# A cross-attention kernel on one core: image values and token norms move from the opening into step 11 of the first batch, and the spread of the image values over heads becomes four whole-row copies

## The reference

```python
text_ehs, ip_ehs = ctx[:, :-4], ctx[:, -4:]
q = heads(x @ W_q); k_t = heads(text_ehs @ W_k); v_t = heads(text_ehs @ W_v)
probs_t = softmax(q @ k_t.T * Dh**-0.5);  text_out = probs_t @ v_t
k_ip = heads(ip_ehs @ W_k_ip);  v_ip = heads(ip_ehs @ W_v_ip)
qsem = l2norm(probs_t @ text_ehs);  ip_n = l2norm(ip_ehs)
fused = q @ k_ip.T * Dh**-0.5 + 0.5 * (qsem @ ip_n.T)
probs_ip = softmax(fused) * spatial_mask[:, None]
out = (text_out + probs_ip @ v_ip) @ W_out + b_out + x
```

## Time and profile before

| what | value |
|---|---|
| time, median of 3 runs | 732.73 us (730.79 to 734.06) |
| profiled execution, its own time | 731.94 us |
| its span | 730.1 us |
| granted TensorE clock, mean | 0.997 of full speed |
| PE busy | 713.3 us (98%) |
| DVE, ACT, POOL busy | 634.2 (87%), 558.5 (76%), 422.1 us (58%) |
| chain of waits, by engine | PE 91%, DVE 2%, DMA 2% |

### The profile page before, as it was taken

The page is one execution under the profiler, slowest core; times in us unless marked ns, Lnnn a source line. Parts: engine busy times, 40 slices in busy tenths (PEclk is TensorE's granted clock), DMA queues, the critical chain, the costliest instruction groups (busy, mean ns, idle before and its releaser), DMA issues.

```text
span 730.1 us, 22544 instructions
## 1 busy us (share of the span) xinstructions
PE 713.3 (98%) x7221; PEld 560.9 (77%) x7221; DVE 634.2 (87%) x1878; ACT 558.5 (76%) x1595; POOL 422.1 (58%) x524
## 2 busy tenths in 40 slices
PE   8898999999999999999999999999999999999897
PEld 6577788787787878788787777878787887877665
DVE  5588998989889898988999898898989989898986
ACT  5478787877878788787877878787887878777772
POOL 7545646465564745656565565656556564654754
PEclk9999999999999999999999999999999999999999
DMA  9764372442536246263543436354352725325001
GB/s 277 164 142 99 79 140 73 83 125 45 120 75 135 74 62 144 41 128 75 107 104 58 105 80 133 76 88 113 51 117 73 142 71 92 64 43 123 13 1 22
DMA packets 136355, 68.57 MB, mean 94 GB/s; under 512 B 76672, under 2 KB 136112, under 8 KB 136240
## 3 DMA queue, kind: packets, MB, share of 16 engines
q1 hardware_dynamic: 131856, 64.05, 41.1%
q10 hardware_dynamic: 4064, 2.73, 1.3%
q0 software_dynamic: 320, 0.36, 0.4%
HBM read 40.38 MB, written 15.24 MB: 76 GB/s over the span
## 4 chain that ended last, share of the span: by engine, by line
PE 91%; DVE 2%; DMA 2%; ACT 1%; issue 1%; POOL 1%; SPq 0%; ACTq 0%; DVEq 0%; POOLq 0%
PE ps_gram L785 18%; PE ps_prep L673 18%; PE ps_pT L768 13%; PE ps_gram L786 12%; PE ps_score L760 6%; PE ps_prep L734 5%; PE ps_val L794 4%; PE ps_val L795 2%; PE ps_prep L731 1%; PE ps_prep L704 1%; PE ps_prep L706 1%; PE ps_prep L824 1%; PE ps_prep L835 1%; DMA w_raw<-in_L_xattn_W_k_ip 1%; DMA q_st<-q_bounce 1%
## 5 line engine op out<-in xcount | busy, mean ns | idle before, releaser
L592 POOL TENSOR_TENSOR dual<-prob 128x371 f32<-128x371 f32 (+1 forms) x288 | 251.3, 872 | 288.1 <-ACT prob L1043 288.1
L785 PE MATMUL ps_gram<-gram_hi,pT_hi 125*128 125x371 f16 (+1 forms) x864 | 272.3, 320 | 0.1
L786 PE MATMUL ps_gram<-gram_lo,pT_hi 125*128 125x371 f16 (+2 forms) x864 | 230.1, 267 | 0.0
L1037 ACT ACTIVATE pT_hi<-ps_pT 125x384 f16<-125x384 f32 (+1 forms) x288 | 138.9, 482 | 113.5 <-PE ps_pT L768 105.4
L1235 DVE TENSOR_TENSOR pT_lo<-ps_pT,pT_hi 125x384 f16<-125x384 f32 (+1 forms) x288 | 155.2, 539 | 33.0 <-ACT pT_hi L1037 28.2
L1027 ACT ACTIVATE prob<-ps_score,low 128x371 f32<-128x371 f32 (+1 forms) x288 | 165.3, 574 | 21.6 <-DVE low L1230 16.4
L1230 DVE TENSOR_REDUCE low<-ps_score 128x1 f32<-128x371 f32 (+1 forms) x288 | 154.9, 538 | 18.8 <-PE ps_score L760 13.7
L1248 DVE CUSTOM_DVE_ANT_0 quad_junk<-ps_gram,dual 128x371 f32<-128x371 f32 (+1 forms) x288 | 153.1, 532 | 4.5 <-PE ps_gram L786 1.6
L794 PE MATMUL ps_val<-val,pT_hi 125*128 125x84 f16 (+3 forms) x864 | 152.3, 196 | 0.0
L1043 ACT ACTIVATE prob<-prob 128x371 f16<-128x371 f32 (+1 forms) x288 | 151.5, 526 | 0.0
L768 PE MATMUL ps_pT<-ident,prob 128*125 128x128 f32 (+1 forms) x864 | 142.2, 273 | 6.5 <-ACT prob L1027 3.2
(11 more groups left out here) (264 smaller groups left out, 1468.4 us busy)
## 6 DMA issues: line engine op xcount, KB each, us to landing
ctx_sb<-in_ctx_t SPq DMA_DIRECT2D x15, 750.0 KB, 5.0
w_raw<-k_bounce SPq DMA_DIRECT2D x32, 216.0 KB, 4.0
k_st<-k_bounce SPq DMA_DIRECT2D x28, 216.0 KB, 3.8
k_bounce<-k_hi SPq DMA_DIRECT2D x15, 288.0 KB, 4.3
k_bounce<-k_lo SPq DMA_DIRECT2D x15, 288.0 KB, 4.4
q_st<-q_bounce SPq DMA_DIRECT2D x60, 63.0 KB, 2.4
xt_sb<-in_x_t SPq DMA_DIRECT2D x16, 168.0 KB, 4.7
w_raw<-k_hi SPq DMA_DIRECT2D x32, 84.0 KB, 3.1
```

The source lines that it names most:

```text
L592: nc.gpsimd.tensor_tensor(dual[0:r, t % 2, :], prob[0:r, g % 4, 0:TX], prob_16[0:r, t % 2, :], ALU.subtract).then_inc(s_dual, 1)
L785: nc.tensor.matmul(ps_gram[t % 2][:, 0:TX], hi, gh[0:TROWS[i], i, :], start=(i == 0), stop=False, skip_group_check=True)
L786: last = nc.tensor.matmul(ps_gram[t % 2][:, i * TC:TX], hi, gl[0:TROWS[i], i, i * TC:TX], start=False, stop=(i == NT - 1), skip_group_chec ...
```

## The change

- Opening: the loads of `W_v_ip`, of the token rows and of `W_out`, the clearing of `vip_diag`, the sums, the inverse root, the diagonal, the image values, the broadcast and the two copies are gone from it. One small reduction on DVE makes `own_head` (80 x 20: one where the head is the row's own).
- Batch 0: SP issues the three loads in step 1 (`W_v_ip` into a quarter of `w_raw` that `k_st` doesn't cover). DVE makes the sums in step 7, POOL the root in step 8, DVE the diagonal in step 9. In step 11 PE makes the broadcast and the image values between transposes and products, in `ps_prep[1]`, after piece 5 and ahead of piece 7 of the next batch; DVE copies them out ahead of its quadratic form. SP writes `vip_rows` to DRAM in step 12.
- The spread: four DMAs instead of 20. Each brings for 4 batches the whole rows of all heads into all 20 head places, 80 partitions of 5,120 bytes. They are issued in steps 16 and 17 of batch 0 and steps 1 and 5 of batch 1.
- POOL multiplies the rows of a batch with `own_head`, in place: batch 0 in step 7 of batch 1 (there it waits for all four spreads), batch n in its own step 8, batch 15 in step 9 of batch 14. `finish` waits for this in place of the spreads.

```diff
-VIP_AT = {9: 5, 10: 5, 11: 5, 13: 5}
+VIP_STEP, VIP_KEEP_STEP, IP_SUM_STEP, IP_ROOT_STEP, IP_DIAG_STEP, LATE_LOAD_STEP, VIP_OUT_STEP = 11, 8, 7, 8, 9, 1, 12
...
+VIP_AT = {(0, 16): 0, (0, 17): 1, (1, 1): 2, (1, 5): 3}
...
-            def spread_v_ip(h0, h1):
+            def spread_v_ip(i):
                 sp.wait_ge(s_vip_out, 16)
...
-                for h in range(h0, h1):
-                    sp.dma_start(vip_diag[h * NIP:(h + 1) * NIP, :, h * DH:(h + 1) * DH],
-                                 vip_view[:, :, h * DH:(h + 1) * DH]).then_inc(s_vip_in, 16)
+                sp.dma_start(vip_diag[:, rows_, :].rearrange("p b c -> p (b c)"),
+                             src.unsqueeze(0).to_broadcast([H, NIP, VIP_SLICE * C])).then_inc(s_vip_in, 16)
+
+            def late_loads():
+                load_rows(sp, wo_sb, w_out, s_wo)
...
+                sp.dma_start(w_v_ip_sb, w_v_ip.rearrange("(c p) n -> p c n", p=P)).then_inc(s_w[3], 16)
+                sp.dma_start(ip_rows[:, :], ip[:, :]).then_inc(s_ip, 16)
...
-            nc.gpsimd.memset(vip_diag[:, :, :], 0.0).then_inc(s_pool_set, 1)
...
+            def keep_own_head(n):
+                if n == 0:
+                    pool.wait_ge(s_vip_in, 16 * len(VIP_AT))
+                    pool.wait_ge(s_own_head, 1)
+                mine = vip_diag[:, n, :].rearrange("p (h d) -> p h d", d=DH)
+                nc.gpsimd.tensor_tensor(mine, mine, own_head[:, :].unsqueeze(2).to_broadcast([H * NIP, H, DH]), ALU.mult).then_inc(s_vip_own, 1)
...
                     end_early(b, t, prepare)
...
+                    if b.n == 1 and t == VIP_KEEP_STEP - 1:
+                        keep_own_head(0)
+                    if b.n and prepare and t == VIP_KEEP_STEP:
+                        keep_own_head(b.n)
...
-            pe.wait_ge(s_setup_ev, 2)
-            pe.wait_ge(s_w[3], 16)
-            for e in range(EC // 2):
-                v_ip(e)
             scores(start, 0)
             scores(start, 1)
-            for e in range(EC // 2, EC):
-                v_ip(e)
             transposes(start, 0)
             scores(start, 2)
-            pe.wait_ge(s_ipdiag, 1)
-            nc.tensor.matmul(ps_prep[1][0:S, 0:64], ones[:, :], ip_diag[:, :], start=True, stop=True).then_inc(s_setup_pe, 1)
+            def image_values():
+                pe.wait_ge(s_prep_lo, NM + VIP_BANK_PIECES_DONE)
+                pe.wait_ge(s_ipdiag, 1)
+                pe.wait_ge(s_w[3], 16)
+                nc.tensor.matmul(ps_prep[1][0:S, 0:64], ones[:, :], ip_diag[:, :], start=True, stop=True)
+                for e in range(EC):
+                    last = nc.tensor.matmul(ps_prep[1][0:64, 64:64 + C], ip_T[:, e, :], w_v_ip_sb[:, e, :], start=(e == 0), stop=(e == EC - 1))
+                last.then_inc(s_setup_pe, 1)
...
+                    if b.n == 0 and t == VIP_STEP:
+                        image_values()
                     products(b, t)
```

More of the change, by code:

```diff
@@ L474, in body @@
                         load_xt(b.next().next())
-                    if b.n == 0 and t == 0:
+                    if b.n == 0 and t == LATE_LOAD_STEP:
+                        late_loads()
+                    if b.n == 0 and t == VIP_OUT_STEP:
                         bring_v_ip()
-                    if b.n == 0 and t in VIP_AT:
-                        done = sum(VIP_AT[at] for at in VIP_AT if at < t)
-                        spread_v_ip(done, done + VIP_AT[t])
+                    if (b.n, t) in VIP_AT:
+                        spread_v_ip(VIP_AT[b.n, t])
                     if prepare and t == Q_OUT_STEP:
@@ L547, in _ @@
             split_lo(start, PIECE_X)
[L548 to L549 removed]
+            nc.gpsimd.memset(q_st[1][:, :, :], 0.0).then_inc(s_pool_set, 1)
             def residual(a):
@@ L1422, in body @@
                         split_wo()
+                    if b.n == 0 and t == IP_SUM_STEP:
+                        ip_sums()
+                    if b.n == 0 and t == IP_DIAG_STEP:
+                        ip_scale()
+                    if b.n == 0 and t == VIP_STEP:
+                        image_values()
                     softly(t, 1)
```

71 lines of the change are left out of this document (42 added, 29 removed).

## The result

| | before | after |
|---|---|---|
| time, median (lowest to highest), 11 runs each | 732.87 us (730.79 to 735.41) | 737.95 us (735.47 to 739.34) |
| ratio, 95% interval | | 1.0065 (1.0046 to 1.0084) |
| profiled execution, its own time and its span | 731.94, 730.1 us | 739.01, 737.2 us |
| granted clock, mean | 0.997 | 0.990 |
| PE busy | 713.3 us | 716.8 us |

The forecast was 731.4 us, "the same", in a range of 728.6 to 734.6. The changed kernel is slower by 5 us. The page's first part hardly tells it: PE has 3.5 us more of busy time and stands idle for some 3.6 us more (the span is longer by 7.1; rows 1 are the same line before).

What follows compares the result with a forecast made beforehand. PE, busy 98% of the span, was taken as the bound. The terms -1.5 - 1.27 + 1.0 + 0.5 + 0.4 gave -0.87, hence 731.1 or 731.9 by two bases; 731.4 us was taken, range 728.6 to 734.6.

Steps and rivals of the forecast that it cites:

- Term 6: POOL: multiplications hidden, but batch 0's waits in batch 1 for the last spread, landing about 102.7 us: plus 0.4 us.
- term 3: Opening: PE's low clock may reach past the start of products 0; plus 1.0 us, bounds 0 and 2.4.
- the third rival: Batch 1: last spread lands late, so POOL, `dual`, DVE and PE stand; +3.7 us, about 736; chance 0.08.
- Term 1: Opening: the query lands earlier with loads and clearing removed; minus 1.5 us, bounds 0 and 3.2.
- Term 2: Opening: the second half of the image values leaves the path, so transposes 0 start earlier; minus 1.27 us.
- the second rival: Opening gives nothing back: query only 0.5 us earlier, PE without filler at 1.2 GHz; +1.5 us, about 733.6; chance 0.22.
- up at 34: Opening: sign that the granted clock of 0.5 reaches past products 0's start and is up at 34 us.
- Term 4: Step 11 of batch 0: image values and broadcast take 2.55 us, mostly covered by 2.00 us idle; plus 0.5 us.
- Term 5: Batch 0: late loads on SP ahead of batch 1's query and keys, with a cover of 3.9 us; costs nothing.

Runs made afterwards that it cites:

- e7: Kernel before with only four whole-row spreads (steps 9, 10, 11, 13 of batch 0), POOL's multiplications and `own_head`, without clearing `vip_diag`; 732.60 us, ratio 0.9986.
- e5: Changed kernel plus 24 unread turns of the identity on TensorE in batch 1's idle time ahead of the transposes; 736.72 us, ratio 1.0040.
- e1: Changed kernel with POOL's multiplications for batches 0 and 1 in steps 10 and 11 of batch 1 instead of 7 and 8; 733.48 us, ratio 1.0014.
- e2: Changed kernel with the fourth spread issued in step 4 of batch 1, ahead of the eight key copies, instead of step 5; 732.83 us, ratio 1.0002.
- e8: e9 with POOL's opening key copies waiting for the query, between text splits and `x` split, and 14 turns ahead of scores 0, not 20; 730.49 us, ratio 0.9967.
- e4: e1 with POOL's four key copies of the opening waiting until the query's and first keys' reads have landed; 735.62 us, ratio 1.0038.
- e3: e1 plus unread turns of the identity in the opening: 20 ahead of scores 0, 7 ahead of transposes 0, 3 behind scores 2; 731.63 us, ratio 0.9984.
- e9: Changed kernel with e2's earlier fourth spread and e3's turns in the opening, without e1's later multiplications; 730.73 us, ratio 0.9973.
- e6: Kernel before with all 8 image-value products and 14 unread turns ahead of scores 0, instead of 4 products ahead and 4 behind; 732.93 us, ratio 0.9989.
- e10: Kernel before with e6's opening and e8's move of POOL's key copies; 732.26 us, ratio 0.9991.

## Why the prediction was wrong, step by step

**Term 6, POOL in batch 1: the step that failed, twice.** It gave +0.4, and batch 1 took +5.87. First the landing. I put the issue at 98.93 and the landing at 102.7, from 1.1 us of transfer at the loads' 359 GB/s and a median landing of 2.6. The issue came at 100.36 (1.06 of that because all of batch 1 came later), and the landing took 5.6 us, against 3.8 in my sum. The median of 2.6 I read wrongly: it is that of the 19 DMAs into `q_st` from 0 to 45 us, and 15 of them are copies of 3.5 KB; the four reads of 63 KB have a median of 3.9 there, and 2.4 in the batches. The profile's page of the kernel before shows how the landing grows with the size, on SP's queue:

```profile
k_st<-k_bounce SPq DMA_DIRECT2D x28, 216.0 KB, 3.8
k_bounce<-k_lo SPq DMA_DIRECT2D x15, 288.0 KB, 4.4
q_st<-q_bounce SPq DMA_DIRECT2D x60, 63.0 KB, 2.4
```

With 288 KB at 4.4 us and the context's 750 KB at 5.0 in the same part of it, an estimate for 400 KB is 4.5 us. From my issue at 98.93 that is 103.4, 1.1 us past the 102.3 at which this term decides: enough to see the wait, if not all of it. And here the 400 KB stood behind eight key copies and in part beside the key bounces. By the windows the DMA engines moved only 112 GB/s at a share of 0.95 at 102 to 103 us, and 213 at a share of 0.63 near the end:

```profile
102.00:103.00 1.00, 1.00 (x11) 0.80 (x10) 1.00 (x4) 0.90 (x4) 0.00 (x0) 1.00 0.95 112
103.00:104.00 1.00, 1.00 (x13) 0.77 (x12) 1.00 (x4) 0.92 (x3) 0.00 (x0) 1.00 0.91 305
...
105.00:105.50 0.50, 0.50 (x9) 0.41 (x7) 0.00 (x0) 0.50 (x2) 0.00 (x0) 1.00 0.63 213
```

A median says what a transfer takes in its usual company; the company of this one was in the trace and I didn't price it. The share of 0.63 at the end would fit 10 busy engines of 16. The Trainium skill says in "DMA: Bandwidth & Descriptors", section "Why a DMA increments its semaphore by 16 and not by 1", that a transfer uses the largest number of engines up to 16 that divides the slowest dimension of both of its sides: here 80 rows and 20 heads, so 10. The trace agrees with its 0.63, and e7 comes near it: its four spreads and a load of `x` (140 KB) are issued by 66.2 us and nothing else before 70.8, and from 68 to 70 us the engines move 199 GB/s at a share of 0.68.

```profile
68.00:70.00 2.00, 2.00 (x22) 1.56 (x21) 1.73 (x7) 1.51 (x5) 2.00 (x3) 1.00 0.68 199
```

So whole-row spreads by themselves run at little over half of the loads' 359 GB/s: 410 KB at 199 are 2.1 us and not 1.1 (an estimate from these two rates). No run tried a form on 16 engines, so the reason stays a reading. By the rule and my own figures it would be an estimate of 1.8 us (359 GB/s times 10/16). By either, the rate is 0.7 to 1.0 of the 1.8 us by which the landing was off, and not all of it.

Second, the wait's price. I had written that a landing of 8.2 us costs 5 us, one for one. That much was right: with batch 1 later by 1.06 the deciding point moves from 102.3 to 103.4, the landing was 2.6 past it, and PE stood for 2.71. But I counted the wait of PE alone. The half clock behind it (2.9 us, e5) doubles it. This was in my own term 3, for the opening, and I didn't carry it to batch 1. With the measured 3.0 and 2.9 the third rival, "PE is held through POOL", to which I gave 0.08, is what happened: it had the mechanism and the place, "from a landing of about 104 us on", and its 736 was 2 below the median measured. Its "slower from a landing of about 104 us on" doesn't follow from its own sum, though: at one for one 104 gives +0.4 us in all, and slower by 0.5% would have taken a landing at 107.3. A landing at 105.98 was enough, because the half clock came on top.

**Term 1, the query earlier: wrong.** -1.5 was taken; it was -0.26, and over the four executions with this opening (changed kernel, e1, e2, e5) it lies between +0.05 and -0.84. The chain of waits of the changed kernel in the opening (rows 4 are its counterpart): the write takes longer, the last read a little less.

```profile
19.86 4.54 DMA q_bounce<-q_lo
...
24.99 4.78 DMA q_st<-q_bounce
```

I had taken off 0.79 MB of loads at their rate. They did free the DMA engines, but not where the query waited: from 18 to 22 us, when it is written, the share falls from 0.97 to 0.75, and yet the write of its low half lands after 4.5 us instead of 3.2. From 22 us on the engines are as full in the changed kernel as before, and only e8, with the key copies gone, empties them. Windows of 22 to 25 and 25 to 30 us, of before, after and e8:

```profile
22.00:25.00 3.00, 3.00 (x24) 2.17 (x23) 0.09 (x1) 0.12 (x1) 2.67 (x5) 1.00 0.85 153
25.00:30.00 5.00, 2.52 (x13) 1.00 (x11) 2.31 (x9) 3.04 (x10) 1.70 (x2) 0.97 0.90 204
```
```profile
22.00:25.00 3.00, 3.00 (x25) 2.16 (x23) 0.00 (x0) 0.00 (x0) 2.33 (x5) 1.00 0.91 163
25.00:30.00 5.00, 1.56 (x13) 0.89 (x10) 2.01 (x7) 3.17 (x10) 0.78 (x1) 1.00 0.89 212
```
```profile
22.00:25.00 3.00, 3.00 (x24) 2.17 (x23) 0.00 (x0) 0.00 (x0) 0.44 (x1) 1.00 0.87 146
25.00:30.00 5.00, 4.29 (x35) 3.43 (x33) 2.82 (x9) 3.40 (x11) 1.25 (x2) 1.00 0.61 156
```

The prediction named the key copies too, without a price of their own, and had them issued 1.5 us earlier. They came at 22.24 instead of 22.72, since POOL, with nothing to clear, waits for the query's high half instead:

```profile
19.93 1.27 POOL L316 DMA_DIRECT2D q_st<-q_hi  x2 [4.25 <-ACT q_hi L1035]
```

e4 and e8 show the key copies to be what counts for the reads: with them out of the way scores 0 come 1.2 us sooner than in the changed kernel and 1.4 sooner than before, by one execution each.

**Term 2** gave -1.27 and was -1.44: the exponential was the next wait, as rows 7 had it.

**Term 3, the clock**, gave +1.0 in bounds of 0 and 2.4 and was +1.78, by e3 the clock alone (2.4 in e1 and e2 and 2.7 in e5, at and above the upper bound). The low clock lay over all of products 0 and the first pieces; products 0 started at 34.43, not at 32.4 as expected, and the clock was at 0.50 from 34 to 36.7 us and not "up at 34". So the three terms of the opening, which were to give -1.8, gave +0.1, as the second rival had it ("gives nothing back", 0.22). Right in mechanism, off in size.

**Term 4** gave +0.5 and was +0.57. The cover of 2.00 us was where rows 9 show it, and PE has no idle time there now.

**Term 5**, the moved DMAs, gave nothing, and no new wait is in batch 0. **Of term 6** the multiplications are hidden, as said: 43.1 us for each later batch.

So the sum was to be -0.87. With what was measured it is +0.1 (opening), +0.6 (step 11) and +5.9 (batch 1): +6.5, and +7.0 with the first loads, which came 0.5 later in this execution. Over the medians it is 5.1: the profiled execution of the changed kernel, at 739.01, is 1.1 above its own median, and that of before 0.9 below.

So the 5.87 us of batch 1 are those of one execution. By the medians its repair is worth 4.5 us (e1) and 5.1 (e2), with the runs on different chips.

The chances: 0.83 on "the same" and 0.06 on slower. The point from which term 6 decides, a landing at 102.3, lay 0.4 ahead of my own guess of 102.7, and the guess stood on a median from another transfer. A cover that is already used up in the forecast has no room for an error in it, and 0.08 was too little for that.

## What to carry to other kernels

When an instruction is put on an engine with a wait for a DMA in front of it, price the landing from a transfer of the same size and in the same place of the queue (look at what the median of a tile's DMAs is made of), and count from the issue of what is ahead of it. If the engine holds up work of others, count the wait of TensorE and then, for the stretch behind it, the half clock: here each came to 3 us. The repair costs a number in a table: issue the transfer one step earlier, ahead of the small copies (e2), or put the waiting instruction later (e1).

What stands idle in front of a wait is not always free to be taken away: the image values kept TensorE's clock up in the opening. When they go, something has to take their place, in every wait and not only in the longest (e3, e9 and e8 against e6). Here the clock was worth 1.8 to 2.7 us; taking the image values off the path, 1.7 us less the 0.6 that they cost in step 11.

## What was not expected of the hardware

- **Two splits that meet.** In e4 DVE's pair of text splits takes 4.79 us instead of 1.00. The second of them starts at 31.92 and ends at 36.25. POOL issues its last key copy until 32.5 and then runs two text splits, the `x` split and a `dual` without a gap, from 32.53 to 35.84; DVE's ends as they do. In e8 DVE's pair overlaps only the last 0.35 us of POOL's text splits and the key copies, and takes 1.21. So it is mostly POOL's tensor instructions in a row and not its issues that DVE was held by, as far as these two runs tell; no run moved the splits alone. The Trainium skill says in "SBUF — State Buffer", section "SBUF: two separate sides", that the two engines share a pair of ports as an exclusive lock, for a DVE instruction with two inputs in SBUF, for the whole of an instruction. The traces agree in that the loser stood still; that it stood for four instructions of the other engine is more than one. By the rows DVE's split had started 0.61 us ahead of POOL's first and alone takes about 0.5. So the starts don't say which engine gets its turn, and a part of POOL's last issue in this isn't ruled out.
- **More bytes are not more time.** The row spread brings 1.6 MB of which a twentieth is used, and needs 16 multiplications; it costs nothing (e7: 0.9986, 0.9963 to 1.0008).
- **A full DMA share tells nothing of the rate**: 0.95 of share moved 112 GB/s with the key copies and 305 a microsecond later at 0.91.

## What stays open

Of the fourth spread's 5.6 us the rate by itself is 2.1 (an estimate from e7's 199 GB/s); how the rest divides into the queue ahead of it, the key bounces beside it and what every DMA takes was not taken apart, and a form on 16 engines was not run.

e6's profile is 0.9 us shorter than that of before, and 1.0 shorter than e9's, while its median is 2.2 us above e9's and hardly below before. The table in e6 says why: three of its 12 executions kept the clock, and the profiled one is among them, so the median stands for the kernel. Why the same program keeps the clock in one execution and loses it in the next is open. Among executions that kept it, e9's ten (median 730.6 us) are 0.4 us below e6's three (731.0), too little and too few to say that moving the image values to step 11 is worth anything once the opening is filled. No run has e9's turns with the image values left in the opening. The versions with them in step 11 and with turns, e9 and e8, are faster than the kernel before, by 0.27% and 0.33%; those that leave them in the opening, e6 and e10, are not shown to be.
